# In a state-space and mixture-of-experts kernel, pieces of the FFN on TensorE go behind the spread of C instead of ahead of it

## What is computed

```python
x = x + 0.5 * ffn(layernorm(x))        # ffn: sum over the 2 best experts of gate * (silu(x @ w1) @ w2)
x = x + attn(layernorm(x))             # two mixers, memory_attend after the second
x = x + 0.5 * ffn(layernorm(x))
# the heart of a mixer, for each token t:
dA = exp(delta_t[:, :, None] * A)
h = h * dA + (delta_t * u_t)[:, :, None] * B_t[:, None, :]
y = einsum('bds,bs->bd', h, C_t)
```

## Time and profile before

| | us |
|---|---|
| median of 3 runs | 1719.58 |
| lowest, highest | 1718.62, 1725.28 |
| the profiled execution's own time | 1717.3 |
| its span, first to last instruction | 1715.5 |
| VectorE busy | 1379.7 (80%) |
| TensorE busy | 1330.5 (78%) |
| ScalarE busy | 1278.6 (75%) |
| the eight groups | 113.0 to 1637.0 |

### The profile page before, as it was taken

The page is one execution under the profiler, slowest core; times in us unless marked ns, Lnnn a source line. Parts: engine busy times, 40 slices in busy tenths (PEclk is TensorE's granted clock), DMA queues, the critical chain, the costliest instruction groups (busy, mean ns, idle before and its releaser), DMA issues. The chain is left out here.

```text
span 1715.5 us, 29243 instructions
## 1 busy us (share of the span) xinstructions
PE 1330.5 (78%) x8754; PEld 1195.6 (70%) x8754; DVE 1379.7 (80%) x2184; ACT 1278.6 (75%) x2657; POOL 568.3 (33%) x610
## 2 busy tenths in 40 slices
PE   7867667886888788887878788887888688568778
PEld 7756556776767677776767677776777677457668
DVE  2438798989888898989889898989889797978742
ACT  3259765988889797988889697878789688648722
POOL 1211324153341535154342536153342533132220
PEclk9969866998989899998999899998989899768889
DMA  7206545666676766666676766666676765555731
GB/s 243 61 13 154 112 78 129 139 154 141 143 168 152 165 140 161 145 155 143 139 178 148 165 148 159 143 149 140 137 172 148 164 143 112 96 127 116 165 84 47
DMA packets 143510, 234.88 MB, mean 137 GB/s; under 512 B 13568, under 2 KB 79360, under 8 KB 143232
## 3 DMA queue, kind: packets, MB, share of 16 engines
q0 software_dynamic: 39424, 132.15, 39.5%
q1 hardware_dynamic: 103936, 100.87, 20.6%
HBM read 90.36 MB, written 25.17 MB: 67 GB/s over the span
## 5 line engine op out<-in xcount | busy, mean ns | idle before, releaser
L1527 POOL DMA_DIRECT2D acc<-G x224 | 204.2, 912 | 893.0 <-DMA acc<-G 444.5
L934 ACT ACTIVATE dA<-delta,A 128x255 f32<-128x255 f32 x1024 | 425.7, 495 | 4.7 <-DVE hs L1283 3.7
L1302 DVE TENSOR_TENSOR G<-hs,b_r 128x1024 f32<-128x1024 f32 x224 | 272.3, 1216 | 60.4 <-PE b_r L646 53.0
L1289 DVE TENSOR_TENSOR_SCAN hs<-dA,b_r 128x512 f32<-128x512 f32 x256 | 298.2, 1202 | 22.9 <-PE b_r L635 12.5
L1283 DVE TENSOR_TENSOR_SCAN hs<-dA,dbu 128x1024 f32<-128x1024 f32 x128 | 292.7, 2286 | 14.2 <-ACT dA L934 7.7
L540 PE MATMUL b_out<-w2s,hT 128*128 x1680 | 245.7, 292 | 64.9 <-issue 44.2
L540 PEld LDWEIGHTS b_out<-w2s,hT 128*128 128x128 f32 x1680 | 216.2, 201 | 86.3 <-issue 85.3
L528 PE MATMUL b_h<-xsT,wst 128*128 128x128 f32 x1680 | 241.0, 290 | 8.1 <-ACT hT L872 8.1
L813 ACT ACT_TABLE_LOAD x180 | 230.9, 1283 | 3.9 <-PEq L1655 0.7
L528 PEld LDWEIGHTS b_h<-xsT,wst 128*128 128x128 f32 x1680 | 223.9, 207 | 10.6 <-issue 9.9
L950 ACT ACTIVATE scaled<-duT,dtT 128x256 f32<-128x256 f32 x512 | 217.0, 500 | 0.3
(11 more groups left out here) (170 smaller groups left out, 1991.7 us busy)
## 6 DMA issues: line engine op xcount, KB each, us to landing
acc<-G POOLq DMA_DIRECT2D x224, 512.0 KB
wst<-w_dram SPq DMA_DIRECT2D x234, 256.0 KB, 3.0
xsort<-sorted SPq DMA_DIRECT2D x70, 192.0 KB, 5.6
results<-ys SPq DMA_DIRECT2D x70, 192.0 KB, 3.1
xin<-x_dram SPq DMA_DIRECT2D x8, 256.0 KB, 5.3
sorted<-ys SPq DMA_DIRECT2D x2, 960.0 KB, 7.1
sorted<-xn,posi POOLq DMA_INDIRECT x112
yk<-results,posi POOLq DMA_INDIRECT x112, 4.8
```

The lines of the kernel that those rows point to most:

```text
L934: last = do(dA[j % 4][:, d, k, 1:], delta[b][:, k, 1:], ACT.Exp, scale=A[:, k, s:s + 1])
L1289: V.tensor_tensor_scan(hs[j % 2][:, d, :, :].rearrange("p h t -> p (h t)"), dA[j % 4][:, d, :, :].rearrange("p h t -> p (h t)"), R[u % 2][ ...
L1302: V.tensor_tensor(to[:, :, :, :], hs[j % 2][:, :, :, :], both(C).unsqueeze(2).broadcast_to([P, DP, HALVES, T]), ALU.mult).then_inc(q_G, 1)
L1527: Q.dma_start(acc[b][:, :, :, :].rearrange("p d h t -> p (d h t)"), G[j % NG][:, :, :, :].rearrange("p d h t -> p (d h t)"), accum_op=ALU. ...
```

## The change

In TensorE's four lines of `ORDER`, ten spreads of C that had FFN pieces directly in front of them now stand ahead of these pieces. All else is the same: the instructions, their number, the waits, and the orders of the other engines.

```diff
-        "p1 t0 k0 t1 in t2 p2 k1 t3 p1 t4 p1 k2 xp p1 t5 dt p1 t6 k3 p1 t7 m1 k4 t8 p1 dx p2 m2 k5 t9 p2 t10 m3 "
+        "p1 t0 k0 t1 in t2 k1 p2 t3 p1 t4 k2 p1 xp p1 t5 dt p1 t6 k3 p1 t7 m1 k4 t8 p1 dx p2 m2 k5 t9 p2 t10 m3 "
         "t11 k6 p2 m4 k7 p1",
-        "t0 p1 t1 t2 p2 k0 p1 t3 p2 fturn k1 t4 t5 fgate p3 fcount p2 k2 p3 out t6 k3 p5 t7 turn t8 k4 in k5 t9 "
+        "t0 p1 t1 t2 k0 p2 p1 t3 p2 fturn k1 t4 t5 fgate p3 fcount k2 p2 p3 out t6 k3 p5 t7 turn t8 k4 in k5 t9 "
...
-        "t0 p1 t1 p1 t2 p1 k0 t3 p3 k1 out p1 t4 p1 k2 t5 p1 t6 p1 turn t7 k3 in k4 t8 p1 xp t9 t10 dt k5 p1 t11 "
-        "p3 k6 p1 dx p2 k7",
-        "t0 t1 p3 t2 k0 p2 t3 p2 fturn p2 fgate k1 p1 t4 fcount t5 p2 turng k2 p1 in k3 t6 p4 k4 t7 t8 xp dt k5 "
+        "t0 p1 t1 p1 t2 k0 p1 t3 k1 p3 out p1 t4 k2 p1 t5 p1 t6 p1 turn t7 k3 in k4 t8 p1 xp t9 t10 dt k5 p1 t11 "
+        "k6 p3 p1 dx k7 p2",
+        "t0 t1 p3 t2 k0 p2 t3 p2 fturn p2 fgate k1 p1 t4 fcount t5 p2 turng k2 p1 in k3 t6 k4 p4 t7 t8 xp dt k5 "
```

## The result

| | before | after |
|---|---|---|
| median of 4 runs, us | 1722.05 | 1786.60 |
| lowest, highest, us | 1718.62, 1725.28 | 1779.26, 1787.81 |
| ratio, 95% interval | | 1.0366, 1.0329 to 1.0404 |
| span of the profiled execution, us | 1715.5 | 1786.0 |

Slower, as predicted, but by 64.6 us and not by 39.5, and 7 us past the range, which ended at 1780.

What follows compares the result with a forecast made beforehand. No engine alone bounds the kernel; what counts is which wait ends last at each place. Terms 22.0 + 5 + 3.5 + 2 + 7 = 39.5 us on 1717.3 gave 1756.8, with 2.3 for the median 1759; range 1736 to 1780.

Steps and rivals of the forecast that it cites:

- Slot 3, 22 us: Slot 3: pieces behind `k4`'s wait delay silu, D14, `ys`, `d5` and `s5`; 22.0 us in all, 19 to 25.
- `s5` at K + 9.6: Slot 3, group 4: K is the end of `g3`, which frees the bank; `s5` moves from K + 5.8 to K + 9.6.
- rival (a): Slot 3's loss is partly taken up by VectorE's waits downstream: 9 to 17 us, 1729 to 1737; chance 0.09.
- The clock, 5 us with ends 0 and 10: Slot 3: half clock behind `k4`'s longer wait slows D12 and U14 by some 1.65 us; half taken for six groups.
- slot 0's 7 us: Slot 0: softplus late by 0.8 us, about twice that at half clock, three groups of each; 7 us, ends 2 and 12.
- Rival (d): Half clock follows nearly every lengthened wait, in slots 0 and 2 too: 1785 us; chance 0.03.
- two rows, one at each clock: Trace rows: clock 0.54 behind an idle time of 1.85 us, 1.00 behind 2.35 us; the basis for half chance.
- Slot 2, first half, 3.5 us with ends 0 and 7: Slot 2, `k0` and `k1`: pieces wait for `g0`, making silu, `d2` and `s2` late; 3.5 us.
- The arithmetic for `d2`: Slot 2, first half: `d2` starts at 987.6 instead of 986.62, shifting `s2` by 1.0 us.
- Slot 2, end, 2 us: Slot 2, `k6` and `k7`: `s0` 1.0 us late, taken up by VectorE's 1.88 us `rstd` wait in groups 1 to 5.
- slot 1, zero: Slot 1, `k0` and `k2`: pieces shift 0.3 us; VectorE's sooner spread is lost waiting longer at `k4`; zero.
- The path I named: Slot 0: D0 behind `k2` delays `xp`, `proj`, `dt` by 1.4 us and softplus by 0.8, through ScalarE to slot 1's `k4`.

Runs made afterwards that it cites:

- slot 3 alone, with repeats: Only slot 3's `k4` moved ahead of its pieces, with `t6` made six times, against the kernel before: 1743.11 us, ratio 1.0083.
- first execution of the whole: The changed kernel with all ten moves, as first measured and profiled against the kernel before: 1786.60 us, ratio 1.0366.
- the whole with five repeats: All ten moves, plus repeats of `t6` (slot 3), `t3` and `t11` (slot 2), `t2` and `t4` (slot 0), against the kernel before: 1757.01 us, 1.0175.
- slots 2 and 3 together, with repeats: Moves of slots 2 and 3 only, repeats in the same five places (`t2`, `t4` of slot 0 three times), against the kernel before: 1752.87 us, 1.0145.
- All of slot 2: Only slot 2's five moves (`k0`, `k1`, `k2`, `k6`, `k7`), against the kernel before: 1747.84 us, ratio 1.0110.
- with `t0` moved: Only `k6` and `k7` of slot 2 moved, with slot 3's `t0` put ahead of D5 and U7, against the kernel before: 1739.51 us, 1.0084.
- the second execution: The changed kernel with all ten moves, unaltered, measured again beside the experiments against the kernel before: 1783.86 us, ratio 1.0328.
- Alone both: Only the four moves in slots 0 and 1, against the kernel before: 1730.67 us, ratio 1.0016.
- the whole with three repeats: All ten moves, with `t6` of slot 3 made six times, `t3` of slot 2 four and `t11` of slot 2 five, against the kernel before: 1770.23 us, 1.0244.
- four repeats: The kernel before in its own order, with `t2`, `t4` (slot 0), `t0` (slot 2), `t5` (slot 2) repeated, against itself without: 1723.32 us, 0.9983.

## Why the prediction was right, and where it failed

**The bound and the direction: right.** The spreads at which VectorE waits were mostly not the moved ones (of the moved, a small one of 0.24 us in slot 0 of group 0 was overlooked: eight, 10.9 us). An earlier `k` bought next to nothing, and the pieces were late for ScalarE and through it for VectorE.

**Slot 3, 22 us: right in mechanism, right in the delay of `s5`, too high in time.** Predicted: `s5` at K + 9.6. Measured at the full clock (with repeats): K + 9.9 to 10.1, 25.8 us over the seven groups. D12 started 1.16 us after K, not 0.9. But the time of that kernel (slot 3 alone, with repeats) was up by 14 us only (9 to 20), and slot 3 by 16.9: VectorE's wait for `yk` behind `s5` took up 8.4. The prediction had this as rival (a), 9 to 17 us from slot 3, and set against it that the gathers hang on the same `ys`; that argument held only in part, as the rows of `yk` were delayed by less than VectorE.

**The clock, 5 us with ends 0 and 10: this is the step that failed.** As a term of its own it was priced at one place, `k4`, at half chance; slot 0's 7 us held it in three groups, and slot 2's terms not at all. At `k4` it was 6.5 us. But the granted clock fell behind lengthened waits in slots 2 and 0 too: behind 1.72 us at `k1` of slot 2, behind 2.2 to 2.4 us at `k6` in four of seven groups of the first execution of the whole, and behind 1.93 us at `k2` of slot 0. The repeats, which change nothing but TensorE's idle time, gave back 26 us of 58 (16 to 37). With them the time, 1757.01, lies inside the range; without them it does not.

**The rest of the sum came out by luck in part.** Without the 5 us the sum of the terms is 34.5 us, and the whole with five repeats measured 30 (24 to 37). But slot 3 was 14 of this and not 22, and slots 2 and 3 together, with repeats, 25, which leaves some 11 (with 8 to either side) for slot 2 and not 5.5. Two errors met.

**How it was weighed.** Rival (d), the half clock behind nearly every lengthened wait, stood at 1785 us with a chance of 0.03. The clock term had been read from two rows, one at each clock, and the one at full clock was given as much weight as the other. The Trainium skill, "TensorE: Matmul & The Clock Gate", section "A second HAM failure mode: psum-queue depth-cycling", pointed this way, but was turned into a price at one place only.

**Slot 2, first half, 3.5 us with ends 0 and 7: too low, 12 measured (7 to 17), its clock included.** The arithmetic for `d2` held where its pieces ran at the full clock: in group 4 `s2` came 7.29 us after `g0`, 1.07 later than before, and 1.0 was forecast. At half clock it came 8.6 to 9.7 us after. And the term looked at ScalarE only. `out` stands in TensorE's queue behind the same pieces, and VectorE waits for it directly.

**Slot 2, end, 2 us: too low.** All of slot 2 is 19 us and its first half 12, which leaves 7; with `t0` moved it is 14. `s0` came 1.8 us later per group and not 1.0 (12.5 us in seven groups, from `g5`'s end). The 1.88 us of `rstd` were indeed taken up: in slot 3 of groups 1 to 5 that wait fell from 8.3 us to 1.9. But 7.5 us came back at once at `lg`, for which TensorE was late as well (2.7 in the second execution, where `rstd` was at 2.4). A wait that ends on one engine is a poor reserve if the next wait is for the engine that was delayed.

**Slot 0, 7 us, and slot 1, zero.** Alone both cost 3 us (up to 7). Beside the others it was 17, and with repeats 5, each with an interval of about 10 us to either side. The path I named, `xp` behind D0 to softplus, was there: softplus came 0.5 to 1.2 us later per group at the full clock (0.8 forecast) and 1.0 to 2.7 at the half. What was missed is `t5`, also behind them, and `s3`.

**Open.** That slots 0 and 1 cost more beside the others than alone rests on 0.95% against 0.16%, with intervals of 0.6 and 0.3 points. Why the clock falls in more groups then (`xp` at half clock in six of groups 1 to 7 in the second execution of the whole, in three of the first, in all or part in four before) was not shown. The two executions of the same kernel differ in where they lose, by 11.6 us in slot 0 and by 10.9 in slot 3, so a single trace's split by slot is not to be leant on. And no run puts repeats into slot 2 alone, so its clock and its order are parted only by the difference above.

## What to carry to other kernels

Before work is put behind a wait, list all that stands in that queue behind it, up to the next point where the engine idles anyway, with each one's waiting engine; words that were not moved (`out`, `t5`) were waited for by up to 2.7 and 3.1 us. Work that fills TensorE's wait for a bank is also what keeps its clock: price the half clock at every wait that the change lengthens, not at the longest alone, and test it by repeating a harmless matmul ahead of the wait. A delay on the way is not yet time: 25.8 us at `s5` were 14 at the end. Look up whether the clock fell at a wait or had been low before it. And a large sum of waits for one line says little: here 33 us of it were removed and no time was gained.

## What the runs showed of the hardware

The length of TensorE's wait alone did not decide whether the granted clock fell. With `k0` and `k1` of slot 2 moved it fell, from 1.00 to 0.50, at a wait of 1.72 us in each of three groups, and was at 1.00 behind 1.43 and 1.61 us. In slot 3 alone, repeating two matmuls of a spread six times in the wait (12 records in 1.57 us) left 1.54 us of idle time, and D12 and U14 behind it ran at the full clock in groups 2 to 5; in groups 1 and 3 of the whole with three repeats the same 1.54 us was left, and D12 took 2.07 us, the half clock.

Over the program the mean granted clock was 0.901 before, 0.881 in the whole and 0.904 with five repeats; adding these 480 matmul records (9234 against 8754) made the whole 26 us faster (16 to 37). In the kernel before, four repeats raised the mean to 0.910 and no gain could be told (0.9983, 0.9959 to 1.0007).

The Trainium skill, "TensorE: Matmul & The Clock Gate", section "A second HAM failure mode: psum-queue depth-cycling", describes such swings for matmuls that cycle through PSUM banks. The traces of this case, where one bank is handed back and forth, agree in kind.
